# A graph layer whose second edge matmul goes from three fp32r products to one fp32 product, with the one-hot rows moved to VectorE

## What is computed

```python
h = jnp.maximum(_layernorm(x, axis=-1), 0.0)                     # 6250 x 256
polarity = jnp.clip(edge_attr[:, 0:1], 0.0, 1.0)
e = jax.nn.relu(raw @ W_e1.T + b_e1) @ W_e2.T + b_e2             # raw: 206250 x 64
edge_emb = (e * (polarity + 0.01)) @ W_le.T + b_le
msg = jax.nn.relu(h[src] + edge_emb)
aggr = jax.ops.segment_sum(msg, dst, num_segments=6250)
t = (h + aggr) @ W_g1.T + b_g1
out = x + jax.nn.relu(layernorm(t) * ln_g + ln_b) @ W_g2.T + b_g2
```

## Time and profile before

| | |
|---|---|
| median of 3 timed runs | 2651.49 us (2642.53 to 2654.57) |
| span of the profiled execution | 2700.1 us |
| PE busy (share of the span) | 2298.1 us (85%) |
| PEld busy | 2056.4 us (76%) |
| DVE busy | 2118.3 us (78%) |
| ACT busy | 2147.3 us (80%) |
| POOL busy | 1618.4 us (60%) |
| mean busy share of the 16 DMA engines, by slices | 4 to 5 tenths, 9 in the first |

### The profile page before, as it was taken

How to read it: one execution, slowest core, us unless ns; L and a number is a source line. 1 busy time by engine, 2 the same in 40 slices (tenths; PEclk the granted TensorE clock), 3 DMA queues, 4 the chain that set the end, 5 groups by cost and what they waited for, 6 DMA issues and landing times.

```text
span 2700.1 us, 47557 instructions
## 1 busy us (share of the span) xinstructions
PE 2298.1 (85%) x15528; PEld 2056.4 (76%) x15528; DVE 2118.3 (78%) x4094; ACT 2147.3 (80%) x4927; POOL 1618.4 (60%) x1679
## 2 busy tenths in 40 slices
PE   5788888888988888888888889888888888888887
PEld 4677778777877778777777778777777777777776
DVE  7787887777878777778787777777887787777886
ACT  7788888887878878788888788787887887878885
POOL 7666665665556656556666665656665665656562
PEclk8899999999999999999999999999999999999999
DMA  9444444554444544444454454444544444544441
GB/s 298 123 124 124 127 130 125 128 128 127 124 127 126 129 127 126 127 124 125 126 136 125 126 134 126 127 125 120 135 129 127 124 128 120 133 126 126 126 129 59
DMA packets 139634, 349.56 MB, mean 129 GB/s; under 512 B 35250, under 2 KB 61684, under 8 KB 139380
## 3 DMA queue, kind: packets, MB, share of 16 engines
q0 software_dynamic: 77376, 211.39, 28.5%
q1 hardware_dynamic: 62004, 135.08, 20.6%
HBM read 333.51 MB, written 12.82 MB: 128 GB/s over the span
## 4 chain that ended last, share of the span: by engine, by line
PE 31%; DVE 26%; issue 17%; ACT 12%; another core or an unknown queue 10%; POOL 1%; DVEq 1%; DMA 1%; ACTq 0%; SPq 0%; POOLq 0%
DVE bank L708 10%; DVE hl L698 9%; PE bank L875 6%; PE bank L858 6%; PE bank L856 5%; PE bank L854 5%; ACT hh L597 5%; PE bank L832 4%; DVE mhl L718 3%; PE bank L833 3%; DVE rlo L432 2%; ACT mhl L609 2%; ACT ha L618 2%; POOL x_sba L374 1%
## 5 line engine op out<-in xcount | busy, mean ns | idle before, releaser
L586 POOL DMA_INDIRECT hx<-gather_table,sidx x1612 | 1579.6, 980 | 1032.1 <-issue 401.3
L708 DVE SCALAR_TENSOR_TENSOR bank<-bank,gt,hx 128x256 f32<-128x256 f32 x1612 | 681.1, 483 | 341.7 <-remote 277.6
L858 PE MATMUL bank<-wcr,hl 128*128 128x256 f32 x3224 | 907.5, 281 | 42.0 <-issue 41.9
L854 PE MATMUL bank<-wcr,hh 128*128 128x256 f32 x3224 | 921.0, 286 | 20.0 <-issue 16.8
L856 PE MATMUL bank<-wcr,hh 128*128 128x256 f32 x3224 | 907.2, 281 | 25.3 <-issue 25.3
L609 ACT ACTIVATE mhl<-bank 128x512 fp32r<-128x512 f32 x806 | 476.7, 600 | 387.2 <-DVE bank L708 307.4
L858 PEld LDWEIGHTS bank<-wcr,hl 128*128 128x128 f32 x3224 | 612.7, 190 | 38.7 <-issue 38.7
L856 PEld LDWEIGHTS bank<-wcr,hh 128*128 128x128 f32 x3224 | 613.6, 190 | 32.1 <-issue 21.8
L854 PEld LDWEIGHTS bank<-wcr,hh 128*128 128x128 f32 x3224 | 615.1, 191 | 26.3 <-issue 23.7
L718 DVE SCALAR_TENSOR_TENSOR mhl<-bank,mhl 128x512 fp32r<-128x512 f32 x806 | 542.9, 688 | 85.5 <-ACT mhl L609 47.1
L698 DVE SCALAR_TENSOR_TENSOR hl<-bank,hh 128x512 fp32r<-128x512 f32 x806 | 518.6, 684 | 76.7 <-ACT hh L597 43.6
(11 more groups left out here) (100 smaller groups left out, 952.5 us busy)
## 6 DMA issues: line engine op xcount, KB each, us to landing
raw<-in_attrT SPq DMA_DIRECT2D x402, 256.0 KB
hx<-gather_table,sidx POOLq DMA_INDIRECT x1612
x_sba<-in_x SPq DMA_DIRECT2D x12, 512.0 KB, 8.9
gather_table<-x_sba SPq DMA_DIRECT2D x12, 512.0 KB, 7.4
xt<-in_x SPq DMA_DIRECT2D x48, 128.0 KB
out<-xt SPq DMA_DIRECT2D x48, 128.0 KB
dst_i<-in_dst_m SPq DMA_DIRECT2D x1, 805.5 KB
sidx<-in_src_m SPq DMA_DIRECT2D x1, 805.5 KB
```

The lines of the kernel that those rows point to most:

```text
L586: eng.indirect_dma_start(out=hx[:, u % NX, j, :], out_offset=None, in_=tables, in_offset=bass.IndirectOffsetOnAxis(ap=sidx[:, t:t + 1], ax ...
L708: last = eng.scalar_tensor_tensor(out=b, in0=b, scalar=gt[:, t:t + 1], in1=hx[:, u % NX, 2 * q + j, :], op0=ALU.mult, op1=ALU.add)
L854: eng.matmul(o, hh[:, u % 2, k, e0:e0 + P], wcr[:, 0, k, :], start=False, stop=False, skip_group_check=seeded)
L858: last = eng.matmul(o, hl[:, u % 2, k, e0:e0 + P], wcr[:, 0, k, :], start=False, stop=(j == 1 and k == 1), skip_group_check=seeded)
```

## The change

Three parts.

1. The second layer multiplies hh, now plain fp32 and not split, with wc in fp32: one matmul in place of three for each block and half. `hl`, `hidden_low`, `wcr` and `r_hl` go. The first layer's bank is free, and the second layer may start, when ACT has written hh (`r_hh`).
2. The one-hot rows are made by DVE in one instruction for a unit: iota is stored negated, and `is_equal` compares it with slot, both broadcast to 128 x 512. It stands behind `raw_low(u+3)`. ACT's `onehot` and `onehot_end` go.
3. ACT seeds both halves of every unit from unit 2 on. PE's c2 matmul stays for units 0 and 1.

```diff
@@ setup, vector
-                eng.tensor_copy(iota[:, :], iota_i[:, :])
+                eng.tensor_scalar(iota[:, :], iota_i[:, :], -1.0, None, ALU.mult)
@@
-                link(eng, eng.tensor_copy(wcr[:, 0, :, :], wc[:, :, :]))
...
-                eng.tensor_tensor(wcr[:, 1, :, :], wc[:, :, :], wcr[:, 0, :, :].bitcast(F32),
@@ edge_path
-                hh = sb("hh", [P, 2, 2, 512], F32R, c)
-                hl = sb("hl", [P, 2, 2, 512], F32R, c)
+                hh = sb("hh", [P, 2, 2, 512], F32, c)
@@
                 def seeds(u):
-                    return u - 1 + u // 2
+                    return 2 * (u - 2)
@@ scalar
                     def seed(u):
                         eng.wait_ge(r_ml, 2 * (u - 2) + 2)
-                        for q in range(u % 2, 2):
+                        for q in range(2):
@@
-                    def onehot(u):
...
-                    def onehot_end(u):
...
@@ scalar, the loop over units
-                        if u >= 1:
-                            onehot_end(u)
                         if u + 3 < UNITS:
                             raw_high(eng, u + 3)
-                        if u + 1 < UNITS:
-                            onehot(u + 1)
-                            if u >= 1:
-                                seed(u + 1)
+                        if 1 <= u < UNITS - 1:
+                            seed(u + 1)
@@ vector
-                    def hidden_low(u):
...
+                    def onehot(u):
+                        if u >= 3:
+                            eng.wait_ge(r_sg, u - 2)
+                        eng.tensor_tensor(oh[:, u % 3, :, :],
+                                          iota[:, :].rearrange("p (a n) -> p a n", a=1).broadcast_to([P, 4, P]),
+                                          slot[:, 4 * u:4 * u + 4].rearrange("p (j n) -> p j n", n=1).broadcast_to([P, 4, P]),
+                                          ALU.is_equal).then_inc(r_oh, 1)
@@ vector, the loop over units
-                        if u + 1 < UNITS:
-                            hidden_low(u + 1)
...
                         if u + 3 < UNITS:
                             raw_low(eng, u + 3)
+                        if u + 1 < UNITS:
+                            onehot(u + 1)
@@ tensor, first_layer
-                        if u < 3:
-                            eng.wait_ge(r_rl, u + 1)
+                        eng.wait_ge(r_rl, u + 1)
@@
-                                eng.wait_ge(r_hl, 2 * (u - 1) + k + 1)
+                                eng.wait_ge(r_hh, 2 * (u - 1) + k + 1)
@@ tensor, second_layer
-                        eng.wait_ge(r_hl, 2 * u + 2)
+                        eng.wait_ge(r_hh, 2 * u + 2)
@@
-                            seeded = u >= 2 and (q == 1 or u % 2 == 0)
+                            seeded = u >= 2
@@
-                                    eng.matmul(o, hh[:, u % 2, k, e0:e0 + P], wcr[:, 0, k, :], start=False, stop=False,
-                                               skip_group_check=seeded)
-                                    eng.matmul(o, hh[:, u % 2, k, e0:e0 + P], wcr[:, 1, k, :], start=False, stop=False,
-                                               skip_group_check=seeded)
-                                    last = eng.matmul(o, hl[:, u % 2, k, e0:e0 + P], wcr[:, 0, k, :],
+                                    last = eng.matmul(o, hh[:, u % 2, k, e0:e0 + P], wc[:, k, :],
                                                       start=False, stop=(j == 1 and k == 1), skip_group_check=seeded)
```

35 lines of the change are left out of this document (5 added, 30 removed).

## The result

The changed kernel takes 2567.01 us (median of 4 runs, 2563.86 to 2570.11), the kernel before 2652.82 us beside it (4 runs, 2642.53 to 2654.57): a ratio of 0.968, 95% interval 0.963 to 0.973. It is faster by 86 us where 206 were forecast; the time lies in the stated range, and in the numbers of rival (a). The profiled execution has a span of 2562.1 us. That is close to the median of its runs, while the traced execution of the kernel before, 2700.1 us, lay 48.6 us over its own; so the two spans differ by 138 us and the two medians by 86.

A forecast was written before the change was run, and what follows sets the result against it. PE was to become the bound at 5.61 us a unit; 0.10 for the clock and 0.29 for stalls made 6.00, 0.51 less than now. Over 403 units that is 206 us: 2651 - 206 = 2445 us, range 2330 to 2610 us.

The forecast's parts named there:

- (a): Rival, chance 0.12: late completions after raw loads still hold PE; 6.3 to 6.48 us a unit, 2565 to 2638 us.
- the new need of 5.61 us: PE's own work a unit after the change: 5.08 us, +0.65 for the fp32 second layer, -0.12 for the c2 matmul.
- the one-hot at 0.69: DVE's new comparison of 128x512 was taken at 0.69 us a unit, after a tensor_tensor of SBUF operands.
- DVE's new need: DVE's work a unit was to fall from 5.16 to 4.56 us, without hl and with the one-hot.
- what remains of stalls: PE's stalls after raw loads and in node units: 0.29 us a unit, a fifth of today's 1.43.
- the clock: 0.10 us a unit added to PE's need, for the time at the lower clock level of 1.2 GHz.
- the starting point: Unit read from an execution of 2700.1 us, 48.6 over the median; the saving of 206 us was taken from 2651.
- The hiding argument: PE has 5.31 us of own work against a circle of 2.3 us, so late completions up to 3.0 us fit in.
- A new wait at nothing: First layer's wait on r_rl in every unit, for a part made three units ahead, was to cost nothing.
- (b): Rival, chance 0.08: POOL is the bound, each one-hot holding a gather for 0.69 us; 6.15 us a unit, 2506 us.
- (c): Rival, chance 0.11: slower, PE's work grows by 0.53 us a unit and its waits do not shrink; 2712 or 2865 us.
- point of decision: For (c): it decides from where PE still waits more than 0.90 us a unit (6.51 - 5.61).

The follow-up runs named there:

- E4: Changed kernel with POOL's gathers two units ahead of PE instead of three; 2338.71 us, 1.039 of the kernel before.
- E7: Kernel before with only the one-hot comparison on DVE and both seeds on ACT, second layer split as before; 2662.66 us, 0.987 of the kernel before.
- E17: Changed kernel with one of the four gathers of a unit left out from unit 4 on; 2347.61 us, 0.870 of the kernel before.
- E9: Changed kernel with two of the four gathers of a unit left out from unit 4 on; 2344.96 us, 0.884 of the kernel before.
- E10: Changed kernel without raw loads after the first three; 2540.31 us, 0.957 of the kernel before.
- E5: The changed kernel itself, run again; 2595.20 us, 0.963 of the kernel before.
- E6: Kernel before with the fp32 second layer alone, one-hot rows and seeds as before; 2619.32 us, 0.972 of the kernel before.
- E8: Changed kernel with DVE's raw low part and one-hot put ahead of the totals; 2579.84 us, 0.957 of the kernel before.
- E2: Kernel before with two of the four gathers of a unit left out from unit 4 on; 2251.14 us, 1.000 of the kernel before.
- E13: Kernel before with two of the four gathers of a unit left out from unit 4 on; 2261.77 us, 0.837 of the kernel before.
- E1: Changed kernel with two of the four gathers of a unit left out from unit 4 on; 2339.27 us, 1.039 of the kernel before.
- E3: Changed kernel without raw loads after the first three; 2338.23 us, 1.038 of the kernel before.
- E16: The changed kernel itself, run again; 2603.67 us, 0.963 of the kernel before.
- E18: Kernel before with one of the four gathers of a unit left out from unit 4 on; 2262.97 us, 0.839 of the kernel before.

## Why the prediction was right and wrong

**Right.** PE's record of 0.216 us, the new need of 5.61 us (5.617 in E4), the one-hot at 0.69, the seeds, DVE's new need (441.45/600 of 6.18 is 4.55 us; 4.56 was forecast). ACT's came out at 3.83 us a unit (372.17/600 of 6.18) for 3.59: the busy times of its groups overlap (before, the six largest add up to 2295 us, and ACT as a whole was busy 2147.3), so taking two groups away frees less than their sum. Nothing waited for it. Faster was right, for the held sessions. POOL's gathers rose from 980 to 1009 ns as summed (0.12 us a unit). In the changed kernel's trace the 460 gathers that overlap a one-hot have a mean of 1163 ns, the others 948. The Trainium skill, page "SBUF — State Buffer", section "SBUF: two separate sides", would have each one-hot stop a gather for up to its length; an estimate by that rule is 0.69 us x 403 = 278 us on POOL in all. Measured, the 460 are longer by 215 ns, 99 us in all, and adding the one-hot to the kernel before (E7) raised the gathers' busy time by 52 us. In E17, where the gathers wait for PE, 390 fall beside a one-hot and take 1350 ns against 945, 158 us in all, nearer to the rule. In the account above the longer gathers are 47 us that the change loses on POOL in the held sessions; under the threshold they cost nothing that shows (E17 2347.61 us, E9 2344.96).

**The step that failed** is the term for what remains of stalls, 0.29 us a unit "after raw loads and in the node units, a fifth of today's 1.43", and with it "PE becomes the bound at 5.61". Measured, 6.18 - 5.61 = 0.57 us a unit is left. It is not a fifth of the old stall but what a pace of 6.1 to 6.2 us leaves, which rows of eight gathers and a pause set. Of it little can be the clock, for which 0.10 was taken: the granted clock is 0.99 in the window 900 to 1500 us, where it was 0.97:

```profile
900.00:1500.00 600.00, 562.47 (x2883) 487.65 (x2883) 441.45 (x847) 372.17 (x729) 392.39 (x388) 0.99 0.50 134
```

The working went wrong at the earlier trace rows: I saw a late completion 3.7 us after a raw load and tied the one to the other, as both come once in two units. The raw load was locked to the same beat and innocent (E10). In the earlier trace rows POOL's gather at 907.83 starts behind the release too, and that was the trace of it: I read POOL as a victim of the late completion, while its row of eight gathers just before, over at 905.30 (907.83 - 2.53), 1.7 us ahead of the release, was what it went with. Counting over all late completions what stood beside each, rather than reading one, would have told the two apart before any run.

**A second term was the starting point.** The 6.51 us a unit were read from an execution of 2700.1 us, and the saving in units was then taken from the median of 2651. From the span it would have been 2700 - 206 = 2494 us. The forecast missed by 122 us: 49 of them are this, and 73 (0.18 x 403) are the unit of 6.18 in place of 6.00.

**The hiding argument** ("late completions of up to 3.0 us fit in") was sound for a delay that doesn't grow. But four of five releases come behind the end of a row, so where rows grow longer the releases come later: DVE's unnamed wait rose from 277.6 to 452.7 us. The rows did grow longer (8.3 gathers on average for 6.0; 7.7 in E5), hence there are fewer pauses, and by the account above that is what the change gains in held sessions. That the rows lengthen because hl's two instructions left the circle is argued from E6 (rows of 8 in 187 cases, 11 of 4) against E7 (153, and 83 of 4), not shown by itself.

**A new wait at nothing**: the first layer's wait on r_rl was said to cost nothing. It is 113.2 us on PEld; moving DVE's part forward (E8) is worth 0.6%, not clearly told from nothing.

**The rivals.** (a) gave the right time, 2565 to 2638, by luck: it wanted 6.3 to 6.48 us a unit, and 6.18 were measured, which by its own conversion is 2518; the 49 us of the starting point made up for it. Its cause is only half right too: a hold remains, but the raw loads don't set it. (b), POOL as the bound by locked ports, did not occur; POOL sets the pace in another way, though it stands 413/403 = 1.0 us a unit in pauses. (c) is what the change does without late completions: PE's work grows by 0.53, and as the kernel before then waits only 0.31 us a unit for anything (5.39 - 5.08), the unit gets 0.23 us longer and the kernel 3.9% slower. Its point of decision, PE still waiting over 0.90 us, was never reached; the slower case came from the other end, a kernel before with nothing left to gain. I had taken the 1.43 us of PE's waiting, from the earlier trace rows, as the kernel's own, and 1.12 us of it (6.51 - 5.39) was gone in E2's session and, by E13, goes with the held completions in a held session too.

**What stays open.** The changed kernel itself didn't run in the quick session; E1, E3 and E4, which leave PE's work as it is, stand for it. It is open what distinguishes a held session from the quick one, on one and the same chip, and by what way gathers hold PE's completions. One thing goes with it: of the semaphore events that the loop's instructions should leave, the traces of the quick session hold all (7250 of 7250 in E4, 8259 of 8259 in E2), those of the held sessions 72% (before), 71% (after), 73% (E16), and 89% where gathers are halved (E9, E13). Of the events of landing DMAs the changed kernel's trace holds 10068 of 34592, E4's 34395. It may be that the recording itself backs up and holds PE. The Trainium skill, page "NOTIFIC — the notification-queue block", section "7.1 Overflow: three behaviours, one of which stalls the engine", says that the block which writes such records pushes back on the engines rather than lose records inside, and that this can throttle an engine. Against it: E17 and E18 lack 20 and 24% of the loop's events too, with next to no loss of time. And the amount to be recorded doesn't decide: without raw loads (E10) there are 28224 landing events to record, without a quarter of the gathers (E17) 28208, and of the changed kernel's 139586 DMA packets E10 has 31842 fewer and E17 19155; yet against the changed kernel E10 gains one per cent and E17 ten. Every run here was recorded, so none shows the kernels without it.

No version beats both kernels everywhere. In held sessions E8's order of the changed kernel has the lowest median of the forms that leave nothing out (0.957), in the quick one the kernel before. Leaving a gather out changes the result, and no form with fewer instructions for the same rows was tried, so the way under the threshold wasn't found.

## What to carry to other kernels

When a wait has no named releaser, gather all its cases and ask which activity each one ends with; two things that come once in the same period can't be told apart by one example. Before crediting a change with an engine's idle time, ask whether the idle time belongs to the kernel or to the conditions of the run, and measure both kernels with the suspected disturber reduced: here it turned 3.2% faster into 3.7% slower (E17 against E18, 2347.61 / 2262.97 = 1.037). And a pacing wait must hang on a count that doesn't itself arrive in bursts.

## What the runs showed of the hardware

- In the traces of the kernel before and the changed one, from held sessions, 36 to 60% of PE's recorded completions came over 0.5 us late, the median of the second layer's second half 1.5 us (before) and 1.8 us (after), with rows of 4 to 12 indirect gathers on POOL; of the recorded ones of ACT and DVE none was late. In the quick session none was late at all, with rows of 12 and 16 gathers (E4). The kernel before takes 18% longer so (2655.53 against 2251.94 us), on the same chip.
- In held sessions there is a threshold: with 4 gathers in a unit whose other work takes 5.6 or 5.4 us, the medians of the changed kernel are 2567 to 2604 us and those of the kernel before 2653 to 2701; with 3 gathers 2348 and 2263 us; with 2 gathers 2345 and 2262.
- A gather of 128 rows took 0.95 us when nothing of DVE's two-operand SBUF work lay beside it and 1.35 us beside the one-hot (E17), with 0.30 us to the next.
- With next to no completion late, PE's records left no gap in 600.00 us of E17, at a granted clock of 1.00.
